# Attention with residual and a causal convolution: the output projection computed as three f32r products of high and low parts

## The reference

```
# x: (16, 512, 1024), mask: (16, 1024), Wq, Wo: (512, 512); 8 heads of 64; all float32
def attention(x, mask, Wq, Wo):
    q = transpose(x) @ Wq.T                         # (B, T, D), used as query, key and value
    scores = scale * q_h @ q_h.T                    # per head, scale = 64 ** -0.5
    logits = (scores * cmask + (1 - cmask) * -1e30) * rmask
    ctx = softmax(logits) @ q_h
    return transpose(concat(ctx) @ Wo.T)
x = x + attention(x, cond, Wq, Wo)
x = x + causal_conv1d(x, cond as taps) + b
```

## Time and profile before

| | us |
|---|---|
| time, median of 3 runs | 4326.45 (4325.39 to 4328.18) |
| the profiled execution's own time | 4327.44 |
| its span | 4325.7 |
| PE busy | 4148.8 (96%) |
| ACT busy | 2850.3 (66%) |
| POOL busy | 2604.2 (60%) |
| DVE busy | 2496.5 (58%) |

### The profile page before, as it was taken

One profiled execution on the slowest core, in us unless ns is written; L12 is line 12 of the kernel. 1 busy time (PEld: TensorE's weight loads), 2 busy tenths in 40 slices (PEclk: granted clock), 3 DMA queues, 4 the chain that ended last, 5 costly groups with the idle time before them and its releaser, 6 DMA issues. The chain is left out here.

```text
span 4325.7 us, 56947 instructions
## 1 busy us (share of the span) xinstructions
PE 4148.8 (96%) x18688; PEld 2982.9 (69%) x18688; DVE 2496.5 (58%) x2259; ACT 2850.3 (66%) x3905; POOL 2604.2 (60%) x1044
## 2 busy tenths in 40 slices
PE   6999999999999999999999999999999999999599
PEld 4776767667676767767676676767676676767398
DVE  4664655556555655656565565656555565656476
ACT  3775767667576766757576676757667675767265
POOL 3775757667575766757576675757567575757200
PEclk8999999999999999999999999999999999999799
DMA  3322333232333333233233323223332422332388
GB/s 98 83 69 59 89 83 93 64 92 66 73 80 78 93 74 83 69 77 85 64 93 74 83 69 93 73 70 84 78 89 62 104 69 59 88 83 54 117 277 270
DMA packets 285135, 385.34 MB, mean 89 GB/s; under 512 B 148915, under 2 KB 216115, under 8 KB 284726
## 3 DMA queue, kind: packets, MB, share of 16 engines
q1 hardware_dynamic: 284854, 381.57, 34.5%
HBM read 112.28 MB, written 67.11 MB: 41 GB/s over the span
## 5 line engine op out<-in xcount | busy, mean ns | idle before, releaser
L579 POOL TENSOR_TENSOR plo<-p,phi 128x1024 fp32r<-128x1024 f32 x1024 | 2598.9, 2549 | 1420.7 <-ACT phi L529 1408.6
L622 DVE TENSOR_REDUCE mrow<-misc 128x1 f32<-128x1024 f32 x1024 | 1214.8, 1217 | 1079.2 <-PE misc L373 1075.1
L527 ACT ACTIVATE p<-sc 128x512 f32<-128x512 f32 x2048 | 1110.6, 594 | 854.1 <-PE sc L410 612.4
L423 PE MATMUL pv<-phi,val 128*128 128x512 f32 x4096 | 1139.0, 400 | 41.5 <-issue 41.5
L529 ACT ACTIVATE phi<-p 128x1024 fp32r<-128x1024 f32 x1024 | 1086.3, 1061 | 32.5
L409 PE MATMUL sc<-quer,keys 128*128 128x512 f32 x2048 | 919.6, 449 | 22.3 <-issue 17.2
L423 PEld LDWEIGHTS pv<-phi,val 128*128 128x128 f32 x4096 | 768.6, 189 | 249.8 <-issue 76.1
L410 PE MATMUL sc<-quer,keys 96*128 96x512 f32 x2048 | 815.3, 398 | 0.0
L427 PE MATMUL pv<-plo,val 128*128 128x512 f32 x2048 | 648.3, 398 | 0.7 <-POOL plo L579 0.7
L373 PE MATMUL misc<-quer,keys 128*128 128x512 f32 x2048 | 596.2, 399 | 22.6 <-DMA keys<-lo 11.6
L409 PEld LDWEIGHTS sc<-quer,keys 128*128 128x128 f32 x2048 | 387.6, 189 | 200.4 <-issue 74.8
(11 more groups left out here) (66 smaller groups left out, 2648.8 us busy)
## 6 DMA issues: line engine op xcount, KB each, us to landing
keys<-hi SPq DMA_DIRECT2D x256, 256.0 KB, 3.1
quer<-mhi SPq DMA_DIRECT2D x256, 256.0 KB, 4.4
xb<-x SPq DMA_DIRECT2D x16, 2048.0 KB, 8.7
keys<-lo SPq DMA_DIRECT2D x128, 256.0 KB, 4.9
quer<-mlo SPq DMA_DIRECT2D x128, 256.0 KB, 3.7
xo<-x SPq DMA_DIRECT2D x64, 512.0 KB, 3.8
x<-xo SPq DMA_DIRECT2D x64, 512.0 KB, 5.0
xin<-x SPq DMA_DIRECT2D x16, 2048.0 KB, 14.2
```

What stands on the lines that cost most here:

```text
L423: pe.matmul(pv[:, half(h)], val[:, i, t, part, :], phi[:, t % NPHI, half(h)], start=(t == 0 and part == 0), stop=False)
L527: act.activation(p32[:, t % NP32, half(h)], sc[:, h, :], ACT.Exp, scale=SCALE).then_inc(s_p32, 1)
L579: pool.tensor_tensor(plo[:, t % NPLO, :], p32[:, t % NP32, :], phi[:, t % NPHI, :].bitcast(F32), ALU.subtract).then_inc(s_plo, 1)
L622: reduced = dve.tensor_reduce(mrow[:, q:q + 1], misc[:, k, :], AX.X, ALU.max)
```

## The change

The output projection's four float32 matmuls of an item become twelve f32r matmuls: for each of the 4 pairs high weights times high context, high weights times low context, low weights times high context. For that `wo` is split once at the start (ACT and DVE), and the context of each pair after the normalisation: ACT copies the high part (`split_context`, after the exponentials of (1, 5)), DVE subtracts it (`context_low`, at (1, 5)). The new arrays need room: `den` has one buffer instead of two, `plo` two instead of four, the two heads' `val` share their columns of ones, `q32` lies in `lo`, and the loaded `wo` lies in `p32` until the batches begin. With one `den` buffer the reciprocals must be done before the pair's own first denominator is copied, so `REC_AT` now puts them at (0, 2): one, (0, 3): two, (0, 4): one, (0, 5): two, (0, 6) and (0, 7): one each, and the multiplication follows at (0, 7).

```diff
-NP32, NPHI, NPLO = 2, 4, 4
+NP32, NPHI, NPLO = 2, 4, 2
-REC_AT = {(0, 5): [0], (0, 6): [1], (0, 7): [2], (1, 0): [3], (1, 1): [4], (1, 2): [5], (1, 3): [6], (1, 4): [7]}
-NORM_AT = (1, 5)
+REC_AT = {(0, 2): [0], (0, 3): [1, 2], (0, 4): [3], (0, 5): [4, 5], (0, 6): [6], (0, 7): [7]}
+NORM_AT = (0, 7)
+SPLIT_AT = (1, 5)
...
-        val = sb("val", [P, 2, KT, 2, P], F32R)
+        val = sb("val", [P, KT, 2, P + DK], F32R)
-        den = sb("den", [P, 2, T], F32)
-        ct = sb("ct", [P, PAIRS, T], F32)
+        den = sb("den", [P, T], F32)
+        ct_hi = sb("ct_hi", [P, PAIRS, T], F32R)
+        ct_lo = sb("ct_lo", [P, PAIRS, T], F32R)
+        wo = p32[:].rearrange("p a (b e) -> p (a b) e", e=D)
...
-                sp.dma_start(wo[:], woT.rearrange("(k p) e -> p k e", p=P)).then_inc(s_const, 16)
+                sp.dma_start(wo, woT.rearrange("(k p) e -> p k e", p=P)).then_inc(s_wo, 16)
...
                 if item[1] == 0:
-                    pe.wait_ge(s_cnorm, PAIRS * (prev_b + 1))
+                    pe.wait_ge(s_ct_lo, PAIRS * (prev_b + 1))
                 for k in range(PAIRS):
-                    last = pe.matmul(out, wo[:, k, m * P:(m + 1) * P], ct[:, k, half(h)],
-                                     start=(k == 0), stop=(k == PAIRS - 1))
+                    w_hi, w_lo = wo_hi[:, k, m * P:(m + 1) * P], wo_lo[:, k, m * P:(m + 1) * P]
+                    pe.matmul(out, w_hi, ct_hi[:, k, half(h)], start=(k == 0), stop=False)
+                    pe.matmul(out, w_hi, ct_lo[:, k, half(h)], start=False, stop=False)
+                    last = pe.matmul(out, w_lo, ct_hi[:, k, half(h)], start=False, stop=(k == PAIRS - 1))
...
             def start():
-                pe.wait_ge(s_const, 32)
+                pe.wait_ge(s_const, 16)
...
             def copy_context(b, p, i):
                 act.wait_ge(s_pv, (head(b, p, i) + 1) * KT)
+                if i == 0 and not (isinstance(b, int) and b == 0 and p == 0):
+                    act.wait_ge(s_cnorm, pair(b, p))
                 if i == 0 and not (isinstance(b, int) and b == 0 and p < 2):
-                    act.wait_ge(s_cnorm, pair(b, p) - 1)
+                    act.wait_ge(s_ct_lo, pair(b, p) - 1)
...
+            def split_context(b, p):
+                act.wait_ge(s_cnorm, pair(b, p) + 1)
+                if p == 0 and not (isinstance(b, int) and b == 0):
+                    act.wait_ge(s_xo, 2 * DT * b)
+                act.activation(ct_hi[:, p, :], ca[:, p % 2, :], ACT.Copy).then_inc(s_ct_hi, 1)
...
             def start():
                 do("start", 0, 0, "pair", PHASES["start"]["pair"], None)
+                act.wait_ge(s_wo, 16)
+                act.activation(wo_hi[:], wo, ACT.Copy).then_inc(s_wo_hi, 1)
                 do("start", 0, 0, "head", PHASES["start"]["head"], (0, 0, 0))
+                act.wait_ge(s_wo_lo, 1)
...
                             exponentials(b, p, i, t, first)
+                            if (i, t) == SPLIT_AT and not (phase == "first" and p == 0):
+                                split_context(*before(b, p))
...
             def normalise(b, p):
...
-                dve.tensor_tensor(ct[:, p, :], ca[:, p % 2, :], den[:, p % 2, :], ALU.mult).then_inc(s_cnorm, 1)
+                dve.tensor_tensor(ca[:, p % 2, :], ca[:, p % 2, :], den[:], ALU.mult).then_inc(s_cnorm, 1)
+
+            def context_low(b, p):
+                dve.wait_ge(s_ct_hi, pair(b, p) + 1)
+                dve.tensor_tensor(ct_lo[:, p, :], ca[:, p % 2, :], ct_hi[:, p, :].bitcast(F32), ALU.subtract).then_inc(s_ct_lo, 1)
...
                 for part in parts:
                         stage(0, 0, part)
+                dve.wait_ge(s_wo_hi, 1)
+                dve.tensor_tensor(wo_lo[:], wo, wo_hi[:].bitcast(F32), ALU.subtract).then_inc(s_wo_lo, 1)
...
                                 if (i, t) == NORM_AT:
                                     normalise(*before(b, p))
+                                if (i, t) == SPLIT_AT:
+                                    context_low(*before(b, p))
```

More of the change, by code:

```diff
@@ L108, in build_attention @@
         wq = sb("wq", [P, DT, D], F32)
-        wo = sb("wo", [P, PAIRS, D], F32)
+        wo_hi = sb("wo_hi", [P, PAIRS, D], F32R)
+        wo_lo = sb("wo_lo", [P, PAIRS, D], F32R)
         ident_r = sb("ident_r", [P, P], F32R)
@@ L115, in build_attention @@
         off8 = sb("off8", [KT, P], F32R)
-        q32 = sb("q32", [P, T], F32)
         hi = sb("hi", [P, T], F32R)
         lo = sb("lo", [P, T], F32R)
+        q32 = lo[:].bitcast(F32)
         mhi = sb("mhi", [P, T], F32R)
@@ L169, in build_attention @@
         s_cnorm = sem("s_cnorm")
+        s_ct_hi = sem("s_ct_hi")
+        s_ct_lo = sem("s_ct_lo")
+        s_wo = sem("s_wo")
+        s_wo_hi = sem("s_wo_hi")
+        s_wo_lo = sem("s_wo_lo")
         s_ones = sem("s_ones")
@@ L422, in context @@
                     for part in range(2):
-                        pe.matmul(pv[:, half(h)], val[:, i, t, part, :], phi[:, t % NPHI, half(h)],
+                        pe.matmul(pv[:, half(h)], val[:, t, part, DK * i:DK * i + P], phi[:, t % NPHI, half(h)],
                                   start=(t == 0 and part == 0), stop=False)
@@ L426, in context @@
                 for h in range(2):
-                    last = pe.matmul(pv[:, half(h)], val[:, i, t, 0, :], plo[:, t % NPLO, half(h)],
+                    last = pe.matmul(pv[:, half(h)], val[:, t, 0, DK * i:DK * i + P], plo[:, t % NPLO, half(h)],
                                      start=False, stop=(t == KT - 1))
@@ L444, in start @@
             def start():
-                pe.wait_ge(s_const, 32)
+                pe.wait_ge(s_const, 16)
                 pe.wait_ge(s_ident, 3)
-                pe.wait_ge(s_ones, 4)
+                pe.wait_ge(s_ones, 2)
                 do("start", 0, 0, "pair", PHASES["start"]["pair"], None)
@@ L502, in values @@
                     act.wait_ge(s_pv, (head(*nxt) - 1) * KT)
-                at = DK * nxt[2]
-                act.activation(val[:, nxt[2], :, :, at:at + DK],
+                at = P * nxt[2]
+                act.activation(val[:, :, :, at:at + DK],
                                misc[:, k, :].rearrange("p (k c d) -> p k c d", c=2, d=DK), ACT.Copy).then_inc(s_val, 1)
@@ L511, in copy_context @@
                 act.wait_ge(s_pv, (head(b, p, i) + 1) * KT)
+                if i == 0 and not (isinstance(b, int) and b == 0 and p == 0):
+                    act.wait_ge(s_cnorm, pair(b, p))
                 if i == 0 and not (isinstance(b, int) and b == 0 and p < 2):
-                    act.wait_ge(s_cnorm, pair(b, p) - 1)
+                    act.wait_ge(s_ct_lo, pair(b, p) - 1)
                 mine, other = slice(DK * i, DK * i + DK), slice(DK - DK * i, P - DK * i)
                 act.activation(ca[mine, p % 2, :], pv[mine, :], ACT.Copy)
-                act.activation(den[mine, p % 2, :], pv[other, :], ACT.Copy).then_inc(s_cab, 1)
+                act.activation(den[mine, :], pv[other, :], ACT.Copy).then_inc(s_cab, 1)
+            def split_context(b, p):
[3 more added lines that the diff above has]
+                act.activation(ct_hi[:, p, :], ca[:, p % 2, :], ACT.Copy).then_inc(s_ct_hi, 1)
             def exponentials(b, p, i, t, first):
@@ L553, in end @@
                 copy_context(B - 1, PAIRS - 1, 1)
+                split_context(B - 1, PAIRS - 1)
             run(act, start, batch, end)
@@ L567, in constants @@
                 pool.tensor_copy(ident_r[:], eye).then_inc(s_ident, 1)
[L568 to L571, removed]
+                pool.memset(val[:, :, 0, DK:P].bitcast(F32), 1.0).then_inc(s_ones, 1)
+                pool.memset(val[:, :, 1, DK:P].bitcast(F32), 0.0).then_inc(s_ones, 1)
             def split(b, p, i, t, first):
@@ L650, in reciprocals @@
                     dve.wait_ge(s_cab, head(b, p, 1) + 1)
-                d = den[:, p % 2, tok(part)]
+                d = den[:, tok(part)]
                 dve.reciprocal(d, d).then_inc(s_rden, 1)
@@ L705, in end @@
                 normalise(B - 1, PAIRS - 1)
+                context_low(B - 1, PAIRS - 1)
                 for item in PHASES["end"]["out"]:
```

## The result

The changed kernel takes 4441.9 us (median of 4 runs, 4439.96 to 4446.68) against 4326.49 for the kernel before (4 runs, 4325.39 to 4328.18): a ratio of 1.0267, 95% interval 1.0251 to 1.0282, so 115 us slower. The prediction was 4321 in a range of 4285 to 4360: wrong, outside the range. The profiled execution took 4440.87, its span is 4439.1.

The account below looks back on a forecast made before the run. PE, busy 96%, was taken as the bound. A batch: items -3.9, items 2 and 3 +1.7, "mt" +1.9, split +0.25, about -1 over fifteen; with start -3 and end -2, -6: 4321 us, range 4285 to 4360.

Parts of the forecast that it names:

- Two `plo` buffers: POOL's wait for PE's context n - 2: 0 in pairs 0, 2 and 3, bound 0.5 us a pair; matters in pair 1.
- rival (e): In pairs 0, 2 and 3 `lo` loses against POOL, "mt" is 2.2 us later still: 4420 us; chance 0.10.
- Items: Output projection on PE, twelve f32r matmuls an item: each item saves 0.65 us, 5.2 a batch, 83 in all.
- "mt" in pairs 0, 2 and 3: PE's "mt" waits for DVE's maxima behind moved reciprocals: 0.95 us late, 0.63 stays, +1.9 a batch.
- Pair 1: `lo` comes behind POOL; output item 3 starts at 1370.9 instead of 1368.55 and ends 1.7 us later, own saving included.
- Split: ACT's copy of the context's high part makes exponentials late: +0.12 us in two pairs, +0.25 a batch.
- Rival (d): POOL goes before DVE's multiplication at (0, 7) of pair 1: +2.05 us a batch, 4352 us; chance 0.15.
- Start and end: Start, PE's wait for loads: -3 us. End, behind the last context, longer split against eight items' saving: -2 us.

Follow-up runs that it names:

- after_pool_late: The changed kernel with three increments of an unused semaphore on POOL behind its wait for `phi` at (0, 2): 4329.5 us, ratio 1.0002.
- before_waits_swapped: The kernel before with POOL's two waits of a step in the other order, first for the context, then for `phi`: 4380.0 us, ratio 1.0121.
- after_rec01: The changed kernel with three reciprocals at (0, 1) and none at (0, 2) to (0, 4): 4322.6 us, ratio 0.9983.

## Why the prediction was wrong

**The step that failed** stands under "Two `plo` buffers": for pairs 0, 2 and 3 "I count 0", and in rival (e) "Nothing upstream of these two changes, which speaks against it". The 0.01 us between 1434.50 and 1434.51 were seen, the price of losing it was worked out at 2.2 us a pair and 4420 in all, and it got a chance of 0.10. Upstream of POOL was an arithmetic instruction that a buffer count of four puts behind the wait for `phi` and a count of two doesn't. It could have been seen without a run from the instructions with their waits beside them; the order of the instructions alone, which stands above, shows what moves and not what each one waits for.

Point by point:

- **Items:** forecast -0.65 each. The steps (0, 0) and (0, 2) of pair 1 went from 10.13 to 9.50 and from 6.71 to 6.08: -0.63. Right, and the f32r matmuls stood 0.23 us apart, not at the 131 ns of the Trainium skill ("TensorE: Matmul & The Clock Gate", "Back-to-back issue gap").
- **"mt" in pairs 0, 2 and 3:** forecast +0.63 net, with `lo` in its place. after_pool_late has +0.99 - 0.32 = +0.67. Right in the kernel where its condition holds; in the changed one it is +2.8 and more (in pair 3 3.14, less 0.20 at (0, 7) and 0.12 at (1, 0)), and (e) gave 0.63 + 2.2 = 2.83. The mechanism of (e) was priced right (2.16 measured, 9.03 against the 6.87 of after_pool_late, for its 2.2) and its chance was not.
- **Pair 1:** the forecast has item 3 start 10.77 us after `mhi`, measured 10.67, and the steps (0, 4) + (0, 5) thus 2.35 longer with the item's own saving in it. Measured at full clock: 2.65 longer in (0, 4) (10.58) and 0.39 shorter in (0, 5) (2.37 against 2.76), together 2.26. Right. In the mean (0, 4) is 3.46 longer, and the difference of 0.81 is the clock.
- **The clock:** counted nowhere. With pair 3's 9.02 as the undisturbed value, pair 0 loses 0.56 a batch, pair 2 0.12 and pair 1 0.81: 1.5 a batch and 22 us in all. This is an estimate from the step lengths. The granted clock bears it out: in the steps (0, 4) + (0, 5) it is 0.82 in pair 0 of all 12 middle batches, in pair 2 of the 3 in which they take over 9.4 us, and 1.00 in pair 3 of all; over the whole run it is 0.979 against 0.990. The two pairs in batch 5, columns as above:

```profile
1333.06:1342.63 9.57, 7.44 (x26) 5.50 (x25) 9.42 (x9) 4.14 (x7) 6.30 (x3) 0.82 0.67 152
1530.34:1539.36 9.02, 6.12 (x26) 4.35 (x25) 8.87 (x8) 4.47 (x7) 6.75 (x4) 1.00 0.70 160
```

- **Split:** forecast +0.25 a batch; step (1, 7) of pair 2 takes 2.42 against 2.41. Nearly 0.
- **Rival (d),** the multiplication at (0, 7) of pair 1: it took 1.23 at 1421.68, POOL started at 1421.77. It did not occur in that batch, by 0.09 us, nor in another (1.22 to 1.23 us in all 15 that have output items). That it stayed out by so little is luck.
- **Start and end:** forecast -3 and -2, measured -4.0 and -1.0. The wait for the mask now ends at 13.1 where that for `wo` ended at 15.9.

The account: 3 x 15 x 2.16 = 97 for `lo`, 22 for the clock, 3 for items that save 0.63 instead of 0.65 and other small parts of the steps, 15 x 0.25 = 4 less for the split, together 118 on a forecast of -6: +112, where the two profiled executions differ by 113.4.

The Trainium skill ("SBUF — State Buffer", "SBUF: two separate sides") says that of DVE and POOL whoever starts first holds the shared ports for the whole instruction. The trace agrees: `lo`'s 3.44 us are POOL's 2.40, less its 0.07 of head start, and 1.1 of its own. The rule was applied rightly; which of two that come within 0.01 us would start first is what the prediction got wrong.

## What to carry to other kernels

Where operations of two engines that exclude each other come within 0.1 us of each other, the old trace doesn't tell the new order: it was the same in every middle batch of a kernel here, but any edit that adds or removes an instruction before one of them, even a buffer count that changes the form of a threshold, can turn it. Price both outcomes and give neither a small chance, or settle the order by a semaphore wait (here worth 139 us, for 0.2 us a pair). Compare the waits of each instruction, and not only their order, when a count or an offset changes. And look whether the engine that waits runs at a full clock behind the new wait.

## What was unexpected on this chip

- One instruction on a register behind a semaphore wait is some 0.07 us (POOL 0.16 after `phi` against 0.08), and was worth 52 us in before_waits_swapped.
- A reciprocal of 128 columns does not wait for POOL nor hold it up: at 1473.82 in the changed kernel it took 0.94 beside a running subtraction of POOL, where `lo` took 3.44; and POOL's subtraction took its free 2.40 beside two of them in the kernel before.
- Behind two waits of 2 us, the granted clock fell in some batches and not in others, with waits of equal length: 12 matmuls in 2.90 or 4.40 us. What makes the difference between the batches stays open; no run here tells it. In after_rec01, where the two waits are 1.2 us, it fell in none of the 12 middle batches.
